# A graph layer on one core: gathered messages summed with destinations as rows, two of four chunks split into two fp32r parts

## What is computed

```python
xn = _layernorm(x, axis=-1)
x = x + _L0_gnn_ref(xn, ...) + _L0_mix_ref(xn[None], ...)[0]
x = x + _L0_ffn_ref(_layernorm(x, axis=-1)[None], ...)[0]
...
all_msg = jnp.einsum('nf,rfo->rno', h, weight)
msg = all_msg[rel_type, src] * norm
gate = jax.nn.sigmoid(all_gate[rel_type, src])[:, None]
agg = jax.ops.segment_sum(msg * gate, dst, num_segments=n_nodes)
return jax.nn.relu(agg)
```

## Time and profile before

| | us |
|---|---|
| median of 3 runs (lowest, highest) | 1845.69 (1840.63, 1846.52) |
| the profiled execution's own time | 1843.73 |
| its span, first to last instruction | 1841.9 |
| TensorE busy | 1782.1 |
| VectorE busy | 1174.5 |
| GpSimd busy | 779.8 |
| ScalarE busy | 772.6 |

### The profile page before, as it was taken

One profiled execution on the slowest core, in us unless ns is written; L12 is line 12 of the kernel. 1 busy time (PEld: TensorE's weight loads), 2 busy tenths in 40 slices (PEclk: granted clock), 3 DMA queues, 4 the chain that ended last, 5 costly groups with the idle time before them and its releaser, 6 DMA issues.

```text
span 1841.9 us, 30480 instructions
## 1 busy us (share of the span) xinstructions
PE 1782.1 (97%) x11088; PEld 1596.9 (87%) x11088; DVE 1174.5 (64%) x3496; ACT 772.6 (42%) x1429; POOL 779.8 (42%) x816
## 2 busy tenths in 40 slices
PE   7999999999999799999789999999999999999998
PEld 5887888888888699998779999999999998999998
DVE  6555555444444667677557676786777777768765
ACT  5555666555554433333024333343332432433443
POOL 2000000000000366767777666666666666676700
PEclk8999999999999999999899999999999999999999
DMA  7665777755555574444433433434334343343410
GB/s 228 240 228 210 279 286 281 270 217 217 217 214 206 210 287 160 148 131 127 150 104 118 131 113 113 123 95 132 110 111 133 100 122 112 99 137 104 121 29 17
DMA packets 113977, 296.06 MB, mean 161 GB/s; under 512 B 18168, under 2 KB 73856, under 8 KB 104484
## 3 DMA queue, kind: packets, MB, share of 16 engines
q1 hardware_dynamic: 75236, 189.63, 27.8%
q0 software_dynamic: 38592, 104.48, 19.6%
HBM read 162.72 MB, written 131.32 MB: 160 GB/s over the span
## 4 chain that ended last, share of the span: by engine, by line
PE 91%; DVE 3%; POOL 2%; issue 1%; ACT 1%; DMA 0%; DVEq 0%; SPq 0%; ACTq 0%
PE bank L51 23%; PE bank L53 22%; PE bank L52 22%; PE bank L1355 17%; POOL plain L596 2%; PE bank L1344 2%; PE bank L1420 1%; PE bank L1248 1%; PE bank L1223 1%; PE bank L1410 1%; PE bank L1401 1%; PE bank L1459 0%; DVE plain L965 0%; DVE plain L841 0%; DVE parts L626 0%
## 5 line engine op out<-in xcount | busy, mean ns | idle before, releaser
L596 POOL DMA_INDIRECT plain<-messages,idxT x784 | 767.4, 979 | 962.2 <-issue 825.3
L51 PE MATMUL bank<-parts 128*128 128x512 f32 (+2 forms) x2232 | 812.7, 364 | 11.6 <-DVE plain L998 5.1
L53 PE MATMUL bank<-parts 128*128 128x512 f32 (+2 forms) x2232 | 785.3, 352 | 0.0
L52 PE MATMUL bank<-parts 128*128 128x512 f32 (+2 forms) x2232 | 784.9, 352 | 0.0
L51 PEld LDWEIGHTS bank<-parts 128*128 128x128 f32 x2232 | 425.3, 191 | 61.4 <-DVE plain L998 6.2
L53 PEld LDWEIGHTS bank<-parts 128*128 128x128 f32 x2232 | 423.8, 190 | 55.2
L52 PEld LDWEIGHTS bank<-parts 128*128 128x128 f32 x2232 | 425.3, 191 | 46.6
L1355 PE MATMUL bank<-plain 128*128 128x128 f32 x3136 | 392.8, 280 | 22.0 <-DMA plain<-messages,idxT 18.3
L1355 PEld LDWEIGHTS bank<-plain 128*128 128x128 f32 x3136 | 377.5, 196 | 28.5 <-DMA plain<-messages,idxT 20.6
L1174 ACT ACTIVATE plain<-bank,small 128x512 f32<-128x512 f32 (+1 forms) x208 | 135.1, 662 | 368.6 <-PE bank L53 365.4
L669 DVE TENSOR_SCALAR plain<-bank,plain 128x256 f32<-128x256 f32 x392 | 171.1, 478 | 163.5 <-PE bank L53 109.8
(11 more groups left out here) (154 smaller groups left out, 976.5 us busy)
## 6 DMA issues: line engine op xcount, KB each, us to landing
messages<-plain SPq DMA_DIRECT2D x49, 2048.0 KB, 7.0
parts<-xnT_scratch SPq DMA_DIRECT2D x20, 1024.0 KB, 5.1
xnT_scratch<-parts SPq DMA_DIRECT2D x98, 128.0 KB, 3.2
plain<-messages,idxT POOLq DMA_INDIRECT x784
w_parts<-parts SPq DMA_DIRECT2D x32, 256.0 KB, 2.4
parts<-w_parts SPq DMA_DIRECT2D x4, 2048.0 KB, 20.3
plain<-in_x SPq DMA_DIRECT2D x48, 128.0 KB, 7.0
plain<-in_x SPq DMA_DIRECT2D x10, 512.0 KB, 4.7
```

What stands on the lines that cost most here:

```text
L51: e.matmul(out, left(0), right(0), start=start, stop=False)
L52: e.matmul(out, left(0), right(1), start=False, stop=False)
L53: return e.matmul(out, left(1), right(0), start=False, stop=stop)
L596: e.indirect_dma_start(msg[:, b % SLOTS, j, :], None, table_rows, bass.IndirectOffsetOnAxis(idxT[:, j, b:b + 1], 0)).then_inc(s_gather[b % ...
```

## The change

- Destinations become the rows of a sum: the selection is stationary, the messages (256 features) move. Each batch covers a fixed window of 128 destinations; batches 2i - 1 and 2i share a window that begins at 64 (i - 1), accumulate in one bank, and are added together to `agg`, now 128 rows x 49 tiles x 256 features. A window that begins in the middle of a tile takes two instructions of 64 rows.
- Of the four chunks of a batch two are split: ScalarE makes the high part of message x edge weight in fp32r (`high_messages`), VectorE the low part (`low_messages`), and the selection of these chunks is plain 0 or 1. TensorE makes two fp32r products for such a chunk. The other two stay f32, with the weight in the selection.
- In step b ScalarE makes the high and VectorE the low parts of batch b + 1. The first two chunks' gathers have their own semaphore, on which ScalarE waits; TensorE waits for the low part, and before its last two chunks for the rest.
- Five slots of gathered messages instead of four.
- The mixture is made with nodes as rows, two tiles at a time, its bias as one more product in the same accumulation. The turns back and ScalarE's copies go; VectorE adds the rectified sum, then x, in place. x and the mixture's input are loaded per pair of tiles.
- The normalisation moves from VectorE to ScalarE, with one small instruction more on VectorE.
- w_out is loaded only when the last `dots` are done. `enough` asks for fewer batches before a group's mixture: before, 1, 5, 4 and 4 batches stand before the mixtures of groups 8 to 11, now 0, 3, 2 and 2. The places of the others are the same.
- In the program of the changed kernel the general path for other edge lists is changed in the same way; it does not run here.

```diff
-LAG = 3
-BASES = 8
...
-SLOTS, HOTS = 4, 3
+SLOTS, HOTS, HIGHS, LOOK = 5, 3, 2, 2
+
+SPLIT, AHEAD_SPLIT = 2, 1
...
-        return BATCHES if START[g + 1] == TILES else -(-START[g + 1] * P * E // N // BATCH) + LAG
+        return min([b for b in range(BATCHES) if ROW0[PAIR_OF[b]] >= START[g + 1] * P] + [BATCHES])
...
-            order.append(("mix_back", g, 0))
-        elif i == 2:
+        elif i == 3 and SIZE[g] > 2:
...
+        msg_low = sb("msg_low", [P, SLOTS, CHUNKS, D], F32R)
+        msg_high = sb("msg_high", [P, HIGHS, SPLIT, D], F32R)
+        onehot = sb("onehot", [P, HOTS, SPLIT, P], F32R)
+        onehot_norm = sb("onehot_norm", [P, HOTS, CHUNKS - SPLIT, P])
...
-            e.dma_start(wout_s, w_out.rearrange("(j p) o -> p j o", p=P)).then_inc(s_wout_in, 16)
...
+                    e.wait_ge(s_dots, TILES)
+                    e.dma_start(wout_s, w_out.rearrange("(j p) o -> p j o", p=P)).then_inc(s_wout_in, 16)
                     e.dma_start(wqT, wqT_dram).then_inc(s_fold_in, 16)
+                    load_mix(0)
...
-                                         bass.IndirectOffsetOnAxis(idxT[:, j, b:b + 1], 0)).then_inc(s_gather[b % SLOTS], 16)
+                                         bass.IndirectOffsetOnAxis(idxT[:, j, b:b + 1], 0)).then_inc(
+                        (s_gather if j < SPLIT else s_gather_rest)[b % SLOTS], 16)
...
-                for j in range(CHUNKS):
-                    m = e.tensor_scalar(onehot[:, b % HOTS, j, :], iota[:, :], offT[:, j, b:b + 1], nrmT[:, j, b:b + 1],
-                                        ALU.is_equal, ALU.mult)
+                e.tensor_tensor(onehot[:, b % HOTS, :, :], iota[:, :].unsqueeze(1).to_broadcast([P, SPLIT, P]),
+                                offT[:, 0:SPLIT, b:b + 1].to_broadcast([P, SPLIT, P]), ALU.is_equal)
+                for j in range(SPLIT, CHUNKS):
+                    m = e.tensor_scalar(onehot_norm[:, b % HOTS, j - SPLIT, :], iota[:, :], offT[:, j, b:b + 1],
+                                        nrmT[:, j, b:b + 1], ALU.is_equal, ALU.mult)
                 m.then_inc(s_onehot, 1)
 
-            def add_batch(b):
...
-                e.wait_ge(s_sum_batch, b + 1)
-                if b:
-                    e.wait_ge(s_add_batch, b)
+            def low_messages(b):
+                e.wait_ge(s_msg_high, b + 1)
+                for j in range(SPLIT):
+                    m = e.scalar_tensor_tensor(msg_low[:, b % SLOTS, j, :], msg[:, b % SLOTS, j, :], nrmT[:, j, b:b + 1],
+                                               raw(msg_high[:, b % HIGHS, j, :]), ALU.mult, ALU.subtract)
+                m.then_inc(s_msg_low, 1)
+
+
+
+            def add_pair(i):
+                e.wait_ge(s_sum_batch, min(2 * i + 1, BATCHES))
+                if i:
+                    e.wait_ge(s_add_pair, i)
                 else:
                     e.wait_ge(s_zero_dve, 2)
                     e.wait_ge(s_zero_act, 2)
-                if b and mixes_done[b] > mixes_done[b - 1]:
-                    e.wait_ge(s_xT_made, relus[mixes_done[b] - 1])
-                cols = agg[:, :, bass.ds(base[b], WINDOW)]
-                e.tensor_tensor(cols, cols, bank[b % 2][:, 0:D].rearrange("p (h n) -> p h n", h=KH), ALU.add).then_inc(s_add_batch, 1)
+                t, row = divmod(ROW0[i], P)
+                spans = [(0, P, t)] if row == 0 else [(row, P, t), (0, row, t + 1)]
+                for r0, r1, t_ in spans:
+                    if t_ < TILES:
+                        m = e.tensor_tensor(agg[r0:r1, t_, :], agg[r0:r1, t_, :], bank[i % 2][r0:r1, 0:D], ALU.add)
+                m.then_inc(s_add_pair, 1)
...
+            def add_mix(g, p):
+                k0, k1 = 2 * p, min(2 * p + 2, SIZE[g])
+                t0 = START[g]
+                rows_ = agg[:, t0 + k0:t0 + k1, :]
+                e.wait_ge(s_mix_sum, mix_use["mix", g, p] + 1)
+                e.wait_ge(s_add_pair, last_pair["mix", g, p])
+                e.scalar_tensor_tensor(rows_, rows_, 0.0, bank[3][:, 0:(k1 - k0) * D].rearrange("p (k o) -> p k o", o=D),
+                                       ALU.max, ALU.add).then_inc(s_misc, 1)
+                e.wait_ge(s_group_x, mix_count(mix_use["mix", g, p]))
+                e.wait_ge(s_misc, misc_use["mix", g, p] + 1)
+                e.tensor_tensor(rows_, rows_, x_in[:, 0:k1 - k0, :], ALU.add).then_inc(s_x_added, 1)
...
-            def norm_tile(g, k):
...
-                e.tensor_scalar(x3[:, k % 2, :], acc[:, g % 2, k, :], mvB[:, k, 0:1], sdB[:, 2, k:k + 1],
-                                ALU.subtract, ALU.mult).then_inc(s_x3, 1)
...
+                        for i in range(LOOK):
                             one_hot(i)
-                    if b + HOTS - 1 < BATCHES:
-                        one_hot(b + HOTS - 1)
-                    add_batch(b)
+                        for i in range(AHEAD_SPLIT):
+                            low_messages(i)
+                    if b + LOOK < BATCHES:
+                        one_hot(b + LOOK)
+                    if b + AHEAD_SPLIT < BATCHES:
+                        low_messages(b + AHEAD_SPLIT)
+                    if b % 2 == 0 or b == BATCHES - 1:
+                        add_pair(PAIR_OF[b])
...
+                    e.wait_ge(s_x2_rstd, 2 * g + 1)
+                    e.scalar_tensor_tensor(sdB[:, 3, 0:SIZE[g]].unsqueeze(2), mvB[:, 0:SIZE[g], 0:1], -1.0,
+                                           sdB[:, 2, 0:SIZE[g]].unsqueeze(2), ALU.mult, ALU.mult).then_inc(s_x2_rstd, 1)
...
+            def high_messages(b):
+                e.wait_ge(s_gather[b % SLOTS], 16 * SPLIT * (b // SLOTS + 1))
+                if b >= HIGHS:
+                    e.wait_ge(s_sum_batch, b - HIGHS + 1)
+                for j in range(SPLIT):
+                    m = e.activation(msg_high[:, b % HIGHS, j, :], msg[:, b % SLOTS, j, :], ACT.Copy, scale=nrmT[:, j, b:b + 1])
+                m.then_inc(s_msg_high, 1)
+
+            def norm_tile(g, k):
+                if k % 2 == 0:
+                    e.wait_ge(s_x2_rstd, 2 * g + 2)
+                if turns_before[g, k // 2]:
+                    e.wait_ge(s_turn_x3, turns_before[g, k // 2])
+                    e.wait_ge(s_acc, turns_before[g, k // 2])
+                e.activation(x3[:, k % 2, :], agg[:, START[g] + k, :], ACT.Identity, bias=sdB[:, 3, k:k + 1],
+                             scale=sdB[:, 2, k:k + 1]).then_inc(s_x3, 1)
...
+                if i == 0:
+                    for k in range(2, SIZE[g]):
+                        norm_tile(g, k)
...
+                elif step == "batch":
+                    if a[0] == 0:
+                        for i in range(AHEAD_SPLIT):
+                            high_messages(i)
+                    if a[0] + AHEAD_SPLIT < BATCHES:
+                        high_messages(a[0] + AHEAD_SPLIT)
...
-                e.wait_ge(s_gather[b % SLOTS], 16 * CHUNKS * (b // SLOTS + 1))
+                e.wait_ge(s_msg_low, b + 1)
                 e.wait_ge(s_onehot, b + 1)
-                if b >= 2:
-                    e.wait_ge(s_add_batch, b - 1)
-                for h in range(KH):
-                    for j in range(CHUNKS):
-                        m = e.matmul(bank[b % 2][:, h * P:(h + 1) * P], msg[:, b % SLOTS, j, h * P:(h + 1) * P],
-                                     onehot[:, b % HOTS, j, :], start=j == 0, stop=j == CHUNKS - 1)
+                i = PAIR_OF[b]
+                first, last = b == 0 or b % 2 == 1, b % 2 == 0 or b == BATCHES - 1
+                if first and i >= 2:
+                    e.wait_ge(s_add_pair, i - 1)
+                for j in range(SPLIT):
+                    e.matmul(bank[i % 2][:, 0:D], onehot[:, b % HOTS, j, :], msg_high[:, b % HIGHS, j, :],
+                             start=first and j == 0, stop=False)
+                    e.matmul(bank[i % 2][:, 0:D], onehot[:, b % HOTS, j, :], msg_low[:, b % SLOTS, j, :], start=False, stop=False)
+                e.wait_ge(s_gather_rest[b % SLOTS], 16 * (CHUNKS - SPLIT) * (b // SLOTS + 1))
+                for j in range(SPLIT, CHUNKS):
+                    m = e.matmul(bank[i % 2][:, 0:D], onehot_norm[:, b % HOTS, j - SPLIT, :], msg[:, b % SLOTS, j, :],
+                                 start=False, stop=last and j == CHUNKS - 1)
...
+            def mix(g, p):
+                e.wait_ge(s_group_xnT, 16 * (mix_use["mix", g, p] + 1))
                 if g == 0:
                     e.wait_ge(s_mix_low, 1)
-                free_misc(("mix", g, h))
-                for q in range(KH):
-                    m = three(e, bank[3][:, 0:n], lambda i: mix_p[:, i, q, h * P:(h + 1) * P],
-                              lambda i: xnT_g[:, i, q, 0:n], q == 0, q == KH - 1)
+                    e.wait_ge(s_bout_low, 1)
+                free_misc(("mix", g, p))
+                for k in range(2 * p, min(2 * p + 2, SIZE[g])):
+                    o = bank[3][:, (k % 2) * D:(k % 2 + 1) * D]
```

(7 more changed lines are left out.)

364 lines of the change are left out of this document (164 added, 200 removed).

## The result

The change makes the kernel slower: 1913.63 us median of 4 runs (1913.19 to 1914.22), against 1844.03 (1840.63 to 1846.52) of the kernel before; ratio 1.0378, 95% interval 1.0366 to 1.039. The forecast was +19.5 us, 1863, with a range up to 1890; measured were +69.6. The direction held, the size did not. In what follows a time without a ratio is the median of that kernel; beside the experiments, but for three runs that are named, the kernel before had medians of 1841 to 1843 us.

The account below looks back on a forecast made before the run. TensorE, busy 97% of the span, was taken as the bound. 1.5 (first batch) - 15 (key stage) - 5 (fold) - 54 (expert stage) + 82 (waits) + 10 (clock) = +19.5 us: 1863 us, range 1800 to 1890.

Parts of the forecast that it names:

- The mixture: Expert stage, TensorE: 3.7 us a group before, 3.4 after; taken as 0.25 us saved a group, 3 us in all.
- The hand-over: Expert stage: TensorE waits for VectorE's low parts, made one batch ahead, at four kinds of places; +82 us, bounds 0 to 110.
- The route's waits: After the logits, VectorE's choice and accumulation delay the low part; TensorE waits up to 5.1 us each, 47 in sum.
- Statistics: After the second mixture pair, VectorE's additions and statistics delay the low part: 2.3 us in 7 groups, 16 us.
- Norm: ScalarE's normalisations and VectorE's small instruction delay casts and low part: 2.85 us in two groups, 0.5 in five, 8 us.
- The first normal turn: ScalarE normalises two further tiles before it casts; TensorE waits 2.7 us in four groups, 11 us.
- The clock's term: Lower TensorE clock after waits: seven long waits cost 1.5 us each, short ones nothing; +10 us.
- The start: Before the expert stage's later groups: first batch +1.5 us, key and value stage -15, fold and first group -5.
- Full gain: Rival, chance 0.13: TensorE never waits because VectorE has a quarter of its time free; 1771 us.
- Half the waits: Rival, chance 0.20: only the route's waits stand, without a loss of clock; 1818 us.
- Gathers as the bound: Rival, chance 0.10: gathers stretch, or ScalarE waiting for them holds up activations; about 1920 us.
- No faster split: Rival, chance 0.05: reloading the selection for high and low part is exposed, a batch stays near 1.7 us; about 1925 us.

Follow-up runs that it names:

- the kernels with 128 rows: Mixture's bias product over 128 rows instead of 33: 1788.34 us on ahead2 with y_add before route (1786.05 with experts' bias too), 1900.38 us on the changed kernel.
- The run with filled waits: The changed kernel with idle fp32r products on TensorE ahead of 18 batches that waited for the low part: 1895.23 us, ratio 1.029.
- ahead2: The changed kernel with high and low parts made two batches ahead instead of one and a third buffer for high parts: 1820.36 us, ratio 0.9877.

## Why the prediction was wrong, point by point

The 82.3 us that the 12 groups lost are: products -35.1 (854.7 to 819.6), waits +93.8 (9.5 to 103.3), clock +23.6. The prediction had -54, +82 and +10. (The 819.6 was had at a clock of 0.99 against 1.00 before, so a few us of clock are still among the products.) So of the 50 us between 19.5 and 69.6 the products' saving, forecast too large, is 19, the clock 14, the waits 12, the start 4.5, and 1.2 lie behind the last route. The mechanism, low parts that come late, was right; what failed are two terms of the sum, the mixture's price and the clock's.

- **The mixture was priced wrong; this is the step that failed for the products.** "Now 28 products of 0.12, 3.4": four of the 28 are the merged bias products of 33 rows, and the tile takes 1.22 us, 4.9 per group. That is 1.5 us per group, 17 of the 19 us missing in this term; the kernels with 128 rows confirm it. The row of one such product didn't exist in the trace of before, but a near one did, the experts' bias of 48 rows, in order of time in the kernel before:

```profile
1323.28 0.39 PE L53 MATMUL bank<-parts 128*128 128x512 f32 x1
1323.60 0.73 PE L1459 MATMUL bank<-parts 48*128 48x256 f32 x4
1324.26 0.38 PE L51 MATMUL bank<-parts 128*128 128x256 f32 x1
1324.48 0.28 PE L52 MATMUL bank<-parts 128*128 128x256 f32 x1
```

It starts 0.09 late, its four take 0.66 instead of 0.48, and the record behind takes 0.22 instead of 0.12. I had not looked at it.
- **The batch was priced right.** It runs from 1422.67 to 1423.83 in the changed kernel, 1.16 us, and the record behind it is 0.18 longer: 1.34, as forecast. That is partly luck: the tail was in neither of my prices, and the 1.71 of before leaves out 0.08 of it. Two key tiles took 5.18 and 5.02 us, forecast 5.06:

```profile
848.46 0.36 PE L1402 MATMUL bank<-msg_high,onehot 128*128 128x256 f32 x1
...
853.64 0.39 PE L1402 MATMUL bank<-msg_high,onehot 128*128 128x256 f32 x1
...
858.66 0.36 PE L1402 MATMUL bank<-msg_high,onehot 128*128 128x256 f32 x1
```

- **The hand-over was right in mechanism and nearly in size.** The route's waits: eight of 4.4 to 6.3 us and two of 1.9, 45.5 together, forecast 47. Statistics: five of 2.73 and two of about 2, 17.6, forecast 16. Norm: two of 3.1 and three of 0.7 to 1.3, 9.3, forecast 8. The first normal turn: four of 2.0 to 3.3, 10.6, forecast 11. Its neighbours, the second turn above all, had four of 1.5 to 1.7, 6.4, and small ones at other places 7.7; both were forecast as 0, and these 14 us are most of the 15 by which the 97 us of waits for low parts exceed 82. About 3 us of waits that the kernel before had in these groups went.
- **The clock's term was too small by 13.6; this is the second step that failed.** I charged seven long waits 1.5 us each, from one row, and nothing for the short ones, from another. The run with filled waits puts it at 23.6. Behind a wait of 5.05 the clock was low for 5.7 us of work, which is 2.85 lost. Short waits can cost too, though not each: all three stretches below begin behind one of 2.73 us.

```profile
965.00:977.00 12.00, 12.00 (x60) 10.97 (x61) 6.78 (x18) 5.73 (x11) 9.26 (x10) 0.75 0.38 108
1379.20:1391.20 12.00, 11.99 (x67) 11.11 (x68) 7.38 (x21) 6.75 (x12) 7.63 (x9) 0.86 0.30 86
1133.10:1142.00 8.90, 8.15 (x50) 7.36 (x51) 7.15 (x21) 4.34 (x9) 5.49 (x6) 1.00 0.28 76
```

- By the Trainium skill (TensorE: Matmul & The Clock Gate, HAM oscillation) each burst after a wait pays again. The prediction's estimate for that was +27 us; the filled waits show 23.6. The trace sides with the page more than with my row, except that some bursts, as the last of these three, pay nothing. That the two figures lie so close is in part luck, since the estimate charged every wait alike.
- **The start** gained 14.0 us where 18.5 were forecast: the first batch waited 5.83 us for its low part (3.66 for its selection before), and the batches at the fold waited for low parts, up to 3.9 us, where they had waited up to 4.6 for gathers.
- **The rivals.** Full gain: false, but ahead2 with 128 rows and the moved accumulation comes near it, 1786 against the 1771 worked out. Half the waits: false, they were all there and more, and the clock with them. Gathers as the bound: false, no wait of TensorE for one stands in the list, and the mean of a gather went only from 979 to 1004 ns; ScalarE waited 12.4 us for gathers, in four pieces. No faster split: false, a batch costs 1.34 (its own terms add up to 1929, not 1925).
- **The signs.** TensorE's busy share is 92%, forecast 93. VectorE's work per group rose by 5.4 us (from 52.4 to 57.8, the groups of three tiles included), forecast 5. A group got 6.9 us longer on average (from 72.0 to 78.9), forecast 2.

## What to carry to other kernels

When a step that an engine already did two rounds ahead is replaced by a hand-over one round ahead, read how long the makers' queues are at their worst place, and charge an idle TensorE with more than its wait: in this kernel 93.8 us of waits cost 23.6 more through the clock, a quarter. Here a third buffer of high parts, with the parts made two batches ahead, turned +69.6 into -23 us, and moving the accumulation and taking the bias products over 128 rows made it -56 (1786.05, the fastest). Before putting a product of fewer rows among products of 128, look at a row of such a height in the trace; full height can be the cheaper.

## What was unexpected of the hardware

- A product of 33 rows between products of 128 costs 0.50 us, one of 128 rows 0.12. The Trainium skill (TensorE: Matmul & The Clock Gate, Step-by-step: what each phase is for) says that the row count doesn't matter to the loading of weights and that the loads are pulled ahead where row groups don't conflict or the spare weight buffer is their target. The times show that the height costs where it changes; whether a conflict of row groups is the cause, no run tells.
- Behind a wait of 2.73 us the mean clock of the next 12 us was 0.75 in one place and 0.86 in another, and in a third that of the next 9 us was 1.00.
